# The first batch tile of a fused recommendation kernel: x loaded behind layer 0's operands, the next tile's rows written amid x, and late-loaded vector work moved

## The reference

```
for k in 0, 1, 2:                       # prev = e at first
    z = einsum('bmd,bhd->bdmh', e, prev)          # all products of fields
    t = einsum over (m, h) of z with w[k] + b[k]  # 128 units, per d
    t = t / sqrt(sum over units and d of t * t)   # per sample
    prev = t
features = sum over d of the three t           # 384 per sample
h = relu([features, dense] @ W_top1 + b);  h = relu(h @ W_top2 + b);  y = h @ W_top3
```

## Time and profile before

| | |
|---|---|
| median of 3 runs | 1174.68 us (1174.21 to 1175.94) |
| the profiled execution, its own time | 1175.5 us |
| its span in the trace | 1173.7 us |
| TensorE busy | 1126.3 us, 96% of the span |
| VectorE busy | 974.9 us, 83% |
| GpSimd busy | 869.2 us, 74% |
| ScalarE busy | 126.4 us, 11% |
| moved by DMA | 205.66 MB, mean 175 GB/s |

### The profile page before, as it was taken

One profiled execution on the slowest core, in us unless ns is written; L12 is line 12 of the kernel. 1 busy time (PEld: TensorE's weight loads), 2 busy tenths in 40 slices (PEclk: granted clock), 3 DMA queues, 4 the chain that ended last, 5 costly groups with the idle time before them and its releaser, 6 DMA issues. The chain is left out here.

```text
span 1173.7 us, 21404 instructions
## 1 busy us (share of the span) xinstructions
PE 1126.3 (96%) x7868; PEld 568.9 (48%) x7868; DVE 974.9 (83%) x835; ACT 126.4 (11%) x266; POOL 869.2 (74%) x614
## 2 busy tenths in 40 slices
PE   0689999999999999999999999999999999999999
PEld 0244545455454545545454554545455454545553
DVE  2588989889898988989898898989889898988772
ACT  0001110101011010101101010110101011110102
POOL 6466868788686878868687887868788786856670
PEclk9899999999999999999999999999999999999989
DMA  7957546382754638274563828456382845637010
GB/s 189 372 141 267 156 158 212 107 297 71 261 160 167 209 107 289 71 283 138 171 209 102 291 71 289 132 183 203 110 278 70 298 123 183 207 108 273 1 51 1
DMA packets 97992, 205.66 MB, mean 175 GB/s; under 512 B 47611, under 2 KB 50619, under 8 KB 97974
## 3 DMA queue, kind: packets, MB, share of 16 engines
q1 hardware_dynamic: 90960, 203.16, 51.7%
q0 software_dynamic: 5120, 1.29, 1.1%
q10 hardware_dynamic: 1894, 0.96, 0.4%
HBM read 203.05 MB, written 2.33 MB: 175 GB/s over the span
## 5 line engine op out<-in xcount | busy, mean ns | idle before, releaser
L600 DVE TENSOR_TENSOR z<-t_ps,xb 128x2048 f32<-128x2048 f32 (+1 forms) x352 | 708.1, 2042 | 92.6 <-PE acc L761 68.9
L317 POOL TENSOR_TENSOR sums<-z,sums 128x1024 f32<-128x1024 f32 x192 | 455.3, 2371 | 15.1
L747 PE MATMUL acc<-z,w_sb 128*64 128x512 f32 x1920 | 438.2, 600 | 7.7 <-DVE z L600 7.7
L314 POOL TENSOR_TENSOR sums<-z 128x512 f32<-128x512 f32 x192 | 246.3, 1283 | 200.9 <-DVE z L600 200.7
L761 PE MATMUL mix_ps<-sums,s_sb 128*64 128x256 f32 x1536 | 281.8, 380 | 2.8 <-POOL sums L317 2.7
L747 PEld LDWEIGHTS acc<-z,w_sb 128*64 128x64 f32 x1920 | 138.9, 139 | 243.5 <-issue 222.7
L761 PE MATMUL acc<-z,w_sb 128*64 128x256 f32 x768 | 228.5, 379 | 1.8 <-DVE z L600 1.8
L761 PE MATMUL mix_ps<-z,w_sb 128*64 128x256 f32 x768 | 228.5, 379 | 0.0
L761 PE MATMUL acc<-z,s_sb 128*64 128x256 f32 x768 | 228.4, 379 | 0.0
L761 PE MATMUL p_ps<-z,w_sb 128*64 128x256 f32 x768 | 228.4, 379 | 0.0
L761 PEld LDWEIGHTS mix_ps<-sums,s_sb 128*64 128x64 f32 x1536 | 159.2, 137 | 88.6 <-POOL sums L317 7.6
(11 more groups left out here) (78 smaller groups left out, 408.1 us busy)
## 6 DMA issues: line engine op xcount, KB each, us to landing
xb<-xt SPq DMA_DIRECT2D x80, 768.0 KB, 5.6
xb<-xq SPq DMA_DIRECT2D x96, 512.0 KB, 4.6
xb<-xt SPq DMA_DIRECT2D x96, 512.0 KB, 6.0
xr<-xt SPq DMA_DIRECT2D x47, 468.0 KB
x<-xt SPq DMA_DIRECT2D x15, 234.0 KB
xr<-xt SPq DMA_DIRECT2D x15, 234.0 KB
gathered<-in_table,rows_of POOLq DMA_INDIRECT x160, 2.4
xt<-gathered SPq DMA_DIRECT2D x16, 72.0 KB, 2.3
```

Source lines behind the costliest of these rows:

```text
L314: nc.gpsimd.tensor_tensor(t2, t3, b11, ALU.add).then_inc(sums_ready, 1)
L317: nc.gpsimd.tensor_tensor(t41, b2, t2_twice, ALU.subtract).then_inc(sums_ready, 1)
L600: nc.vector.tensor_tensor(z[:, at:at + n, :], t_ps[k - 1][:, :].rearrange("p (a n) -> p a n", a=1).broadcast_to([P, n, N]), xb[:, XB_ROW[c ...
L747: last = nc.tensor.matmul(acc[k][o, :], w_sb[k][:, field + r, o], z[:, at + r, :], start=(c == 0 and r == 0), stop=(c == NCH - 1 and r == ...
```

## The change

There are three edits, all for tile 0. SP waits for all four groups of layer 0's operands before it issues the first chunk of x. It writes the rows of tile 1, plain and mixed, after issuing chunk 5 (`NCH // 2`) of tile 0's x in place of after w2. DVE does the first part of `mixed_weights(2, ...)` after the products of chunk 9, and for tile 0 all four groups of `products0(1)` and then the other three parts come after the products of chunk 10; other tiles keep their order.

```diff
@@ SP
             sp.wait_ge(xq_written, 16)
+
+            for g in range(len(LOADS0)):
+                sp.wait_ge(xr_loaded[g], 16)
             for c in range(NCH):
                 load_chunk(0, c)
+                if c == NCH // 2:
+
+                    write_rows(1)
+                    write_mixed(1)
             sp.dma_start(w_sb[2][:, :, :], w2.rearrange("(m h) o -> h m o", h=P)).then_inc(w_loaded[2], 16)
-            write_rows(1)
-            write_mixed(1)
             sp.wait_ge(xt_written, 96)
             sp.wait_ge(acc0_ready, 1)
             load_layer0(1)
@@ DVE, tile(i, first, last)
                     if c == 6 and not first:
                         norm_sums(2, i - 1)
-                    if c >= NCH - 4 and first:
-                        mixed_weights(2, c - NCH + 4)
-                    if c == 8 and not last:
+                    if c == NCH - 2 and first:
+                        mixed_weights(2, 0)
+                    if c == 8 and not first and not last:
                         products0(i + 1, (0,))
-                    if c == 10 and not last:
+                    if c == 10 and not first and not last:
                         products0(i + 1, (1, 2, 3,))
+                if first:
+
+                    products0(i + 1, range(len(LOADS0)))
+                    for part in range(1, 4):
+                        mixed_weights(2, part)
                 shared_sums(i, 1)
                 add_shared(i, 1)
```

## The result

The changed kernel takes 1177.80 us (median of 20 runs, 1175.65 to 1181.89); the kernel before, in as many runs beside it, 1174.53 us. The ratio is 1.0032, 95% interval 1.0025 to 1.0040: slower by 3.3 to 3.8 us, where 0.7 us faster was forecast. Single runs far off the others (one of 2032 us of the kernel before, here and again later, and one of 2456 us of edit 3 alone) are left out of the ratios. The profiled execution took 1176.81 us with a span of 1175.0 us.

The account below looks back on a forecast made before the run. TensorE's unbroken run from layer 2 of tile 0 was the bound. DVE 0.6 us sooner, layer 2's start 2.5 us sooner, mostly lost to clock and POOL's sums: 0.7 us gained, 1174.0 us; own range 1172.4 to 1177, 8-in-10 range 1169 to 1178.5.

Parts of the forecast that it names:

- the transfers behind the hole: From mixed rows at 50.9 to w2 at 74.8: 18 rows of x at 406 GB/s, 11.6 us, then w2 9.6 us.
- the hole: SP's load queue empty for some 6.5 us, to 52.8, while write_mixed(1) waits for the mixed rows.
- its own signs: Wrong if the queue has no idle stretch near 46 to 52, or shared sums begin outside 85 to 89.
- What bounds: TensorE's unbroken run from layer 2 of tile 0 on; a change is worth how much that run's start, 95.14, moves.
- Edit 1: Layer 0 of tile 0: operands landed by 30, no pause between matmuls, end at 36.6 against 42.04, 5.5 us gained.
- Edit 2: Tile 1's row writes: plain rows cost nothing; mixed rows, ready at 50.9, hold all loads behind them, emptying the queue.
- Edit 3: DVE's late-loaded work: chunk 10 waits for w2 at 74.8, TensorE idles 4 to 5 us, three combinations take 3.0 us.
- From w2 to the shared sums: DVE from w2 at 74.8, through tile 1's operand products (to 84.0) and three combinations, to shared sums at 87.0.
- The rivals: Faster operands, 1170.5 us (0.18); mixed rows early enough, no empty queue, 1167 us (0.10); slower, 1177.7 us (0.17).
- case C: Layer 0 of tile 0 slow to its end (40.1) or its loads late; shared sums at 90.5, 1177.7 us; chance 0.17.
- What lasts: Of layer 2's 2.5 us earlier start, 1.4 to 2.9 us lost to the clock, POOL's sums limiting too; 0.7 us gained.

Follow-up runs that it names:

- edit 3 alone: Only the reordering of DVE's w2 combinations and tile 1 products, against the kernel before; transfers as before: 1172.35 us, ratio 0.9970.
- the rows mixed early: The whole change, with GpSimd mixing tile 1's rows right behind its gathers and ahead of all sums: 1173.49 us, ratio 0.9992 against the kernel before.
- The fills: The changed kernel plus 14 filling matmuls ahead of chunk 10 and 6 ahead of layer 2: 1182.76 us; with 7 and 2: 1177.15 us.

## Why the prediction was wrong

The mechanism it named is the one that runs. Two terms of its sum were too small, both on the same side, and a third, too large, hid a part of that. The sum stood next to zero, so its sign fell with them. The step that failed is the price of the transfers behind the hole: 23.9 us from the mixed rows to w2, where 27.0 and 28.8 us were measured. By its own signs it was wrong, with the shared sums outside of 85 to 89 (89.06 by little, 92.76 clearly).

- **What bounds**: right. TensorE's run from layer 2 on is unaltered, and the time goes with its start, to within about 1 us: layer 2 at 95.14, 94.71 with 1.75 us of slow pace behind it, 98.42 and 103.23 stand beside spans of 1173.7, 1175.0, 1177.8 and 1181.1 us.
- **Edit 1**: "landed at 29.5 to 31.3, taken 30", and "the pause between the eight and the twenty matmuls goes". SP issued its first chunk at 32.19 and 33.26, 2 to 3 us after the landing I took, and the pause shrank to 1.1 to 2.9 us but did not go. Layer 0's end, forecast 36.6, was 36.98 in one profile and 39 to 41 in the others: the gain is 1 to 5 us, mostly about 2. That 36.98 comes so near is luck: 5.5 us of slow pace had been taken, and no pause; there were 3.7 and 1.26. How long the slow pace lasts does not follow the pause (the twenty matmuls took 4.51 us behind 1.26, and 6.05 behind 1.13 with the rows mixed early); why it differs is open. The rows give the granted clock as 1.00 over layer 0 of tile 0, so its slow pace is read from the matmuls' durations alone. "The wait of SP costs nothing by itself" fails most clearly: it puts 9 us between the old first chunk (23.18) and the new one, and with edit 3 that is 2.8 us of time.
- **Edit 2**: the hole was named with its cause, its place (chunk 6 issued just behind the mixing) and its queue. "The plain rows cost nothing" holds in the change itself only because the mixed rows come later still: SP was held 7.98 us in issuing them, until 48.15, and the mixed rows came at 51.79. With the mixing early it is these writes that hold SP, to 48.65. The earlier trace rows already had the same three writes hold SP for 23.14 us behind a backlog.
- **The transfers behind the hole**: this is the step that failed in size. From mixed rows to w2, forecast 23.9 us (50.9 to 74.8), took 27.0 and 28.8 us in the two profiles of the change, and 25.7 to 26.7 in those of the four other kernels that had edit 2 and the mixing late. The last 18 rows of x were priced at the rate of a queue with a backlog, 406 GB/s or 11.6 us; they took 13.3 us in both profiles. And w2 was there 12.1 and 13.8 us after x's end, where the forecast had 10.4: its price came from a stretch of the earlier trace rows in which only small writes were queued behind w2, and here tile 1's operands took most of the 0.9 and 1.3 MB that moved beside w2. That these loads are what delays w2 is my reading of the bytes: in the four other kernels, with the same loads behind it, w2 was there 10.4 to 11.4 us after x's end, as far as the bytes moved show that end.
- **Edit 3**: right in its parts. Chunk 10 waited for w2 (9.67 us of DVE's, for TensorE 6.14), the three combinations took the short 0.95 us each. By itself it gains 2.7 us, the only edit that gains alone.
- **From w2 to the shared sums**: too long in the forecast, 12.2 us (74.8 to 87.0) against 10.3 and 9.5, since tile 1's operands came sooner behind w2 than taken. That hid 2.0 and 2.7 us of what the transfers had cost: the shared sums, forecast 87.0, began at 89.06 and 92.76, though w2 came 4.0 and 8.5 us late.
- **The rivals**: beyond 89 the text itself had said that case C decides. C is nearest in numbers (1177.7), and in part in its cause: layer 0 did end at 40.1 in the second profile, with the mixed rows at 54.5 (C had 54.4). But it missed the longer transfers (shared sums at 90.5, 92.76 measured) and added a loss to the clock that did not come there. That its sum fits is partly luck.
- **What lasts**: "1.4 to 2.9 us lost to the clock". It was 1.75 in one profile, none in the other, and keeping the clock up gave nothing that could be measured. The chance of 0.17 for slower was too low: most terms had the far end of their range on the slow side (layer 0 +3.5 against -1.0, the combinations up to 3.7), and a chain of such terms should have been centred there.

Three things stay open. Between two profiles of the same kernel, with the same order of issues, w2 came 1.8 us later behind the mixed rows; the drift lies behind x, with more of the following loads moved first, and the runs do not show why. Nor do they show why x is slow at first behind the hole (279 GB/s at a DMA share of 0.96): an empty queue alone does not explain it, as in the same kernel x's first loads, issued at 32.19, ran at 350 GB/s from 34 to 36 us and at 413 from 36 to 38. And with edits 1 and 2 not run without 3, what edit 3 is worth inside the whole change is not known.

## What to carry to other kernels

A small write that waits for another engine, put amid large loads in one queue, holds all that is behind it; ask of each wait on the issuing engine when it is granted at its new place, not at its old one, and move what grants it forward first (here three small instructions, worth some 4 us). When several edits share one queue, try each alone and in pairs, since their worths don't add. Edit 3 alone gave 2.7 us. Edit 1 gave nothing alone, cost 2.8 beside edit 3, and seemed to gain 3 beside both others. Edit 2 cost 10.8 alone, some 10 beside edit 3, and some 3 beside both. And give a load's price a range when what is queued directly behind it changes: the same w2 took 10.4 us with small writes behind it, and between 10.4 and 13.8 with large loads behind it.

## What the runs showed of the hardware that was not expected

SP is not free once it has reached its issue: with much queued ahead, the issue itself lasts. One issue of x behind w2 took 13.85 us, three writes 7.98 us, where the same three took 1.67 us at 128 us in the kernel before, with nothing large queued, and 23.14 at 43.95, until the backlog was through at 67. The Trainium skill ("DMA: Bandwidth & Descriptors", section "Anatomy of one DMA — SWDGE (gpsimd) path") has the issuing sequencer as the one that waits on semaphores, and the hole of 5.4 us at 44 GB/s agrees with it. The long issues are a second way in which SP is held; that they wait for room in the queue is my reading of these rows, no run tests it.

A matmul into one half of the array, repeated into the same half, took 0.86 us in its two records (11.75 us for 27 records, granted clock 1.00), where those that alternate between the halves took 0.44 (6.18 us for 28). The fills also repeat one set of weights and overwrite their result, so that the half is the cause is not isolated.
